# Octonion feed-forward kernel: the low half of one hidden block is rounded on VectorE instead of GpSimd

## The reference

```python
xn = layernorm(x)                          # per row of 1024
def oct_ternary_linear(xp, W):             # weights rounded to -s, 0, s
    Wq = ternary_dequant(W)
    M = einsum('jik,jod->koid', S_OCT, Wq) # 8 x 8 octonion table of signs
    return einsum('...id,koid->...ko', xp, M)
gate, up = oct(xn, w_gate), oct(xn, w_up)  # hidden width 8 x 341.5 -> 2732
h   = silu(gate) * up
ffn = oct(h, w_down)
out = x + autocorrelation_aggregate(xn) + ffn
```

## Time and profile before

| | |
|---|---|
| median of 3 runs | 595.21 us |
| the profiled execution, whole | 595.38 us |
| its span, first to last instruction | 593.3 us |
| TensorE, VectorE, ScalarE, GpSimd busy | 98%, 86%, 60%, 77% |
| mean granted TensorE clock | 0.999 of 2.4 GHz |

### The profile page before, as it was taken

How to read it: one execution, slowest core, us unless ns; L and a number is a source line. 1 busy time by engine, 2 the same in 40 slices (tenths; PEclk the granted TensorE clock), 3 DMA queues, 4 the chain that set the end, 5 groups by cost and what they waited for, 6 DMA issues and landing times.

```text
span 593.3 us, 16442 instructions
## 1 busy us (share of the span) xinstructions
PE 581.7 (98%) x6764; PEld 541.9 (91%) x6764; DVE 510.1 (86%) x1230; ACT 357.0 (60%) x497; POOL 457.5 (77%) x362
## 2 busy tenths in 40 slices
PE   7999999999999999999999999999999999999996
PEld 7999998899989998899989998899989998998996
DVE  4787978889998999979998999979998999958854
ACT  4678896565586555764586555764586555543540
POOL 3407659999689977999689977999689977997920
PEclk9999999999999999999999999999999999999999
DMA  9720120002220203002210113002210201002021
GB/s 211 162 73 1 72 72 2 2 2 72 72 73 1 71 21 126 2 2 73 76 69 1 63 35 121 2 2 72 81 63 2 72 3 72 2 3 72 2 73 72
DMA packets 10251, 30.67 MB, mean 52 GB/s; under 512 B 928, under 2 KB 4032, under 8 KB 10176
## 3 DMA queue, kind: packets, MB, share of 16 engines
q1 hardware_dynamic: 10176, 29.62, 15.7%
HBM read 21.23 MB, written 8.39 MB: 50 GB/s over the span
## 4 chain that ended last, share of the span: by engine, by line
POOL 50%; issue 28%; PE 7%; ACT 1%; DVE 1%; POOLq 0%; ACTq 0%
POOL hop L1371 15%; POOL hs L1365 9%; POOL hs L1361 9%; POOL hs L1366 9%; PE acc L488 5%; POOL hs L1360 5%; PE acc L391 1%; POOL r L1319 1%; ACT pk L627 0%; ACT pk L613 0%; POOL hop L1368 0%; PE acc L384 0%; ACT wd L692 0%; POOL onep L1330 0%; POOL vr L1317 0%
## 5 line engine op out<-in xcount | busy, mean ns | idle before, releaser
L488 PE MATMUL acc<-wd,hop 114*128 114x128 f16 (+1 forms) x2944 | 170.7, 219 | 0.8 <-POOL hop L1371 0.7
L488 PEld LDWEIGHTS acc<-wd,hop 114*128 114x128 f16 (+1 forms) x2944 | 167.4, 98 | 2.0 <-POOL hop L1371 0.9
L711 ACT ACTIVATE pk<-acc 114x512 f32<-114x512 f32 (+1 forms) x120 | 70.9, 591 | 84.4 <-PE acc L384 49.4
L1360 POOL TENSOR_TENSOR hs<-hx 114x512 f32<-114x512 f32 x47 | 60.0, 1277 | 55.4 <-DVE hx L1116 51.7
L1371 POOL TENSOR_TENSOR hop<-hs,hop 114x1024 f16<-114x1024 f32 x46 | 98.4, 2139 | 2.7 <-ACT hop L766 2.7
L1368 POOL TENSOR_TENSOR hop<-hx,hop 114x1024 f16<-114x1024 f32 x46 | 98.4, 2139 | 1.3 <-ACT hop L755 1.3
L384 PE MATMUL acc<-xop,wu 128*128 128x256 f16 x704 | 84.2, 273 | 1.0 <-DVE hx L1116 0.7
L1019 DVE TENSOR_TENSOR bd<-acc,pk 114x256 f32<-114x256 f32 (+1 forms) x104 | 43.5, 418 | 48.3 <-ACT pk L711 48.3
L384 PE MATMUL acc<-xop,wg 128*128 128x256 f16 x704 | 84.2, 273 | 0.1
L391 PE MATMUL acc<-xop,wu 128*128 128x256 f16 x704 | 84.1, 273 | 0.1
L391 PE MATMUL acc<-xop,wg 128*128 128x256 f16 x704 | 84.0, 273 | 0.2 <-DVE acc L1059 0.2
(11 more groups left out here) (168 smaller groups left out, 932.1 us busy)
## 6 DMA issues: line engine op xcount, KB each, us to landing
xr<-in_x SPq DMA_DIRECT2D x16, 512.0 KB, 4.5
zx<-in_x SPq DMA_DIRECT2D x16, 512.0 KB, 3.7
out_y<-zx SPq DMA_DIRECT2D x16, 512.0 KB, 2.6
hop<-in_w_down SPq DMA_DIRECT2D x1, 1364.0 KB, 18.9
hop<-in_w_gate SPq DMA_DIRECT2D x2, 576.0 KB, 9.5
hop<-in_w_up SPq DMA_DIRECT2D x1, 1152.0 KB
hop<-in_w_gate SPq DMA_DIRECT2D x1, 192.0 KB
hop<-in_w_up SPq DMA_DIRECT2D x1, 192.0 KB
```

Source lines behind the costliest of these rows:

```text
L488: last = nc.tensor.matmul(acc[:, bank[n], s // 2, at:at + P], operand(g, c, t, form, level), wd[0:WIDE[c], slot, c, :], start=which == 0 a ...
L711: nc.scalar.activation(pk[0:rows, q % 2, :, :], pair[:, :, T:2 * T], ACT.Copy, scale=XS if u[0] == "X" else 1.0).then_inc(copied, 1)
L1360: nc.gpsimd.tensor_tensor(hs[:, 4:8:2, :], h[:, 0:4:2, :], h[:, 1:4:2, :], ALU.add)
```

## The change

VectorE's program gets one new instruction at step n = 32, ahead of the additions for N(0, 0): the low level of h of block 5. It waits for the high level of that block (`hhi_done`) and for the low level of block 4 (`h_free`), and raises `h_free` in GpSimd's place. In GpSimd's program the subtraction is gone for this one block, and a wait for `h_free` to have reached the count of block 5 stands there; the instruction behind that wait is the low level of the sums of the same block (line 1371 of before, 1382 after). All other blocks are as they were.

```diff
             for n in range(OPEN, N + 2):
                 u = units[n] if n < N else ("",)
                 kind = u[0]
+                if u == ("N", 0, 0):
+
+                    v = ("U", 0, 2, 1)
+                    m = u_no[v]
+                    dve.wait_ge(hhi_done, m + 1)
+                    dve.wait_ge(h_free, m)
+                    nc.vector.tensor_tensor(half_of(0, 2, 4, 1), by_tile(hx[0:CH, m % 4, :, :]), half_of(0, 2, 4, 0), ALU.subtract).then_inc(h_free, 1)
...
-                pool.wait_ge(hhi_done, m + 1)
-                nc.gpsimd.tensor_tensor(half_of(g, c, 4 * Y, 1), by_tile(h), half_of(g, c, 4 * Y, 0), ALU.subtract).then_inc(h_free, 1)
+                if u == ("U", 0, 2, 1):
+
+                    pool.wait_ge(h_free, m + 1)
+                else:
+                    pool.wait_ge(hhi_done, m + 1)
+                    nc.gpsimd.tensor_tensor(half_of(g, c, 4 * Y, 1), by_tile(h), half_of(g, c, 4 * Y, 0), ALU.subtract).then_inc(h_free, 1)
```

## The result

The changed kernel takes 601.68 us (median of 5 runs, 600.53 to 602.06), the kernel before 595.03 us (median of 5, 594.58 to 595.30). The ratio is 1.0109, with a 95% interval of 1.0098 to 1.0120: the change makes the kernel about 6.5 us slower by this ratio (the medians differ by 6.65). The forecast was 601.7.

The account below looks back on a forecast made before the run. The prediction took TensorE, busy 581.7 of 593.3 us, to bound the kernel. To the median of 595.2 it added 4.4 us for the longer pause and 2.1 for the fallen clock, giving 601.7 us, range 599.2 to 602.8.

Parts of the forecast that it names:

- When it runs: VectorE's new instruction, queued behind the second additions for G(1, 1, 0), was to start at 120.89 and end at 122.10.
- The pause: TensorE's idle time before the third chunk of N(0, 0) was to grow from 0.74 to 5.2 us, costing 4.4 us.
- the rival that later slack takes it back: TensorE's later 0.7 us pause would go too and nothing else move: 598.9 us, chance 0.05.
- GpSimd's slack of 3.95 us: GpSimd's waiting at 151.76; claimed not to help, being slack against VectorE's product, which itself follows TensorE.
- The clock: TensorE's clock was to fall 1.2 us before the pause's end; 2.1 us taken, bounds 0 and 2.6.
- a delay of 4.0 us: At the end of the trace, time from last matmuls (588.37) to the clock's fall; applied to the 5.2 us pause.
- Nothing shows a pause above 4.0 us at full clock: Argument against the rival that the pause comes but the clock stays up: 599.6 us, chance 0.35.
- The 2.6 us from the kernel's start: Upper end of the clock's cost, from TensorE's half-rate transposes at the start: about 5.2 us of work at half rate.
- Hold-up: Rival: the new instruction is held up by a GpSimd read or slow for its strides: 603.2 us, chance 0.04.
- the second rule: Two-SBUF-input VectorE and SBUF-reading GpSimd instructions exclude each other; up to 1.5 us, nothing while GpSimd only waits.
- Not slower: Rival: VectorE is in time and the shortened GpSimd chain ends TensorE's pause: 594.5 us if faster; chance 0.04, half faster.
- The deciding point: If VectorE's new instruction ended by 117.6, line 1371 would start no later than now; its end was put at 122.1.

Follow-up runs that it names:

- e1: Against the changed kernel, the new VectorE instruction stands one step earlier, ahead of the additions for G(1, 1, 0); 594.79 us, ratio 0.9997 to the kernel before.
- e6: Against the changed kernel, the new VectorE instruction stands right behind the product of block 6 in step 30; 594.42 us, ratio 0.9987 to the kernel before.
- e7: Against the kernel before, GpSimd keeps the subtraction but waits for a tiny VectorE instruction at the new instruction's place; 599.94 us, ratio 1.0079.
- e5: Changed kernel with 36 float16 matmuls of 256 columns added on TensorE in the pause; 599.22 us, ratio 1.0066 to the kernel before.
- e4: Changed kernel with 24 extra transposes on TensorE between the second and third chunk of N(0, 0); 601.84 us.
- e3: Against the changed kernel, TensorE waits before the third chunk of N(0, 0), GpSimd no longer before block 5's sums; 600.61 us, ratio 1.0093.
- e2: Against the changed kernel, the new instruction stands two steps earlier, ahead of the additions for U(1, 0, 1); 595.74 us, ratio 1.0008 to the kernel before.

## Why the prediction was right

*The path.* The removal frees GpSimd for 2.1 us, and the wait takes back more than that. e1 and e6 show that the place of the instruction decides, e7 that the wait alone makes most of the pause. GpSimd waits from 115.86 to 122.37, 6.5 us as forecast.

*When it runs.* Forecast 120.89, seen 121.08 in an execution that was 0.22 us late as a whole. Its length, 1.21 us, was taken from line 1108 and came out at 1.21. The idle time of VectorE before the additions for N(0, 0) covered it.

*The pause.* Forecast 5.2 us, seen 5.13. The shift stays the same to the end (6.55 us at 130, 6.52 at the last matmuls), so the rival that later slack takes it back is out. GpSimd's slack of 3.95 us before block 9 was of no use: it is 3.96 us afterwards. Only its wait before block 8 has grown, from 0.19 us in the kernel before to 2.16, by 1.97 us:

```profile
138.52 1.28 POOL L1360 TENSOR_TENSOR hs<-hx 114x512 f32<-114x512 f32 x1 [0.19 <-DVE hx L1116]
```

```profile
145.08 1.27 POOL L1367 TENSOR_TENSOR hs<-hx 114x512 f32<-114x512 f32 x1 [2.16 <-DVE hx L1116]
...
158.30 1.28 POOL L1367 TENSOR_TENSOR hs<-hx 114x512 f32<-114x512 f32 x1 [3.96 <-DVE hx L1116]
```

That is the clock's share of 1.98 us seen from the other side: the pause delays GpSimd and TensorE alike, the slow matmuls TensorE alone, and GpSimd then waits for what follows TensorE. The experiments agree: in e5, with the clock up, this wait is 0.22 us; in e4 and e7, where the slow matmuls cost 1.68 us, it is 1.86.

*The clock.* The size, 2.1 us, was right (1.98 by the rows), but the way to it had a wrong step. I read a delay of 4.0 us between the last matmul and the fall from the end of one trace. There is no such fixed delay. The fall came 2.4 us after the last matmul in the changed kernel; in e3 and e7 it came 4.7 and 4.3 us after it, when TensorE had resumed; and at the end of the nine traces it came 1.9 us (e5) to 4.8 us (the changed kernel) after the last matmul. "Nothing shows a pause above 4.0 us at full clock" was no ground for a threshold; a pause of 3.47 us was enough. So it is partly luck that the size fits. The clock was low for 6.8 us, 2.7 of them in the pause, where they cost nothing; in e3, e4 and e7 it was low for 3.4 us, all of them in work, which cost 1.7 us. The 2.6 us from the kernel's start, from which I came down to 2.1, was also one execution's: the same transposes differ by over 1 us between traces. And the sum leaves out that two executions differ by as much, so that 601.7 and 601.68 agree to the last digit is luck too. One of the five runs of the changed kernel, that at 600.53 us, has a mean clock of 0.997 against 0.994 in the others: the clock was low for a shorter time in it. How much of its 1.15 us under the median is the clock's isn't shown.

*Hold-up.* It was right to keep the second rule apart. In the changed kernel the new instruction runs undisturbed, since GpSimd is waiting; where GpSimd was reading (e2, e3, e6) it took 1.88, 1.63 and 1.92 us. In all three it ended 1.1 us after GpSimd's instruction had ended, whenever it had started. GpSimd's next instruction, where it started beside VectorE's (e2, e3), took 2.13 us and again ended 1.1 us after the other. The Trainium skill (SBUF — State Buffer, "Who interferes with whom") says that a VectorE instruction with two SBUF inputs contends with a GpSimd instruction that reads SBUF, and the traces agree.

*Not slower.* The deciding point was given as an end of the instruction at 117.6. In e1 and e6 N(0, 0) starts 0.3 and 0.6 us earlier than in the execution of before, so the point lies at 117.3 and 117.0 there. In e1 the instruction ends at 117.0, just ahead of it, and the time is that of before within its interval; in e6 it ends at 116.1 and the kernel is faster.

## What to carry to other kernels

Work moved to another engine is worth only what its new place in that engine's in-order queue allows. Read when the queue gets there, and read too what stands behind that place and who waits for it (e2). A wait put into the queue of the engine that was to be relieved can cost more than the work taken from it, here 6.5 us for 2.1. A pause of TensorE such as those of 3.5 to 5.1 us here can be paid for twice, once as a pause and once in the clock behind it.

## What the hardware showed that I had not expected

- The clock can fall after TensorE has resumed: in e4 0.2 us after the matmuls had begun again, in e7 0.25 us (at about 122.96) and in e3 1.3 us after. It is then low for 3.4 us. In the changed kernel, where it fell in the pause, it was low for 6.8 us.
- Twenty-four float32 transposes in the pause, 2.84 us by their row, did not keep the clock up (e4); thirty-six float16 matmuls, 4.11 us by theirs, did (e5). The kind of the work, its time and the idle time left (2.26 against 1.00 us) all differ between the two, so which of them matters is open.
- Where GpSimd works without a pause, the meeting of the two engines costs twice in a row: 0.67 us on VectorE, then 0.86 us on GpSimd's next instruction (e2).
